# A Swin block on one core: the four turns of a round set behind each other, the other fillers placed singly

## The reference, cut to what matters

```python
shortcut = x
y = _ln(x, norm1_w, norm1_b)
y = jnp.roll(y, (-SS[0], -SS[1]), axis=(1, 2))
...
qkv = (win @ qkv_w.T).reshape(B * nW, N, 3, h, d).transpose(2, 0, 3, 1, 4)
q, k, v = (qkv[0], qkv[1], qkv[2])
attn = jnp.einsum('bhnd,bhmd->bhnm', q, k) * scale
...
attn = jax.nn.softmax(attn.reshape(B * nW, h, N, N), axis=-1)
out = jnp.einsum('bhnm,bhmd->bhnd', attn, v).transpose(0, 2, 1, 3).reshape(B * nW, N, C)
out = out @ proj_w.T + proj_b
...
x = shortcut + out
z = _ln(x, norm2_w, norm2_b)
z = jax.nn.gelu(z @ fc1_w.T + fc1_b, approximate=False) @ fc2_w.T + fc2_b
return x + z
```

## Time and profile before

| | |
|---|---|
| median of 3 runs | 2226.96 us (2225.48 to 2228.99) |
| the profiled execution | 2222.98 us |
| its span | 2221.2 us |
| granted TensorE clock over the span | 0.991 |
| busy share: TensorE, its weight loads, VectorE, ScalarE, GpSimd | 97%, 75%, 79%, 70%, 80% |

### The profile page before, as it was taken

The page is one execution under the profiler, slowest core; times in us unless marked ns, Lnnn a source line. Parts: engine busy times, 40 slices in busy tenths (PEclk is TensorE's granted clock), DMA queues, the critical chain, the costliest instruction groups (busy, mean ns, idle before and its releaser), DMA issues.

```text
span 2221.2 us, 147938 instructions
## 1 busy us (share of the span) xinstructions
PE 2147.9 (97%) x62756; PEld 1670.2 (75%) x62756; DVE 1748.1 (79%) x3231; ACT 1546.9 (70%) x2435; POOL 1770.5 (80%) x1687
## 2 busy tenths in 40 slices
PE   4999999999999999999999999999999999999997
PEld 3777777777777777777777777777777777777775
DVE  5778887887887888788788788878878887887874
ACT  3577777677677677767767767776776777677675
POOL 5788888888888888888888888888888888888874
PEclk7999999999999999999999999999999999999999
DMA  4232322222323332332333223222223323322321
GB/s 109 64 76 76 76 75 75 76 76 74 77 75 76 75 75 76 73 78 75 76 76 74 76 74 76 75 74 76 75 75 77 73 75 75 75 76 74 77 67 35
DMA packets 178587, 165.86 MB, mean 75 GB/s; under 512 B 21144, under 2 KB 152458, under 8 KB 178074
## 3 DMA queue, kind: packets, MB, share of 16 engines
q1 hardware_dynamic: 178074, 157.60, 28.1%
HBM read 28.99 MB, written 25.77 MB: 25 GB/s over the span
## 4 chain that ended last, share of the span: by engine, by line
PE 83%; ACT 9%; issue 4%; SPq 2%; DVE 1%; DMA 1%; ACTq 0%; POOL 0%; DVEq 0%; POOLq 0%
PE O L749 13%; PE ST L735 10%; PE M L757 9%; PE S L713 9%; PE ST L729 8%; PE M L842 8%; PE M L820 6%; PE M L789 5%; PE M L805 5%; PE M L775 5%; ACT L445 5%; ACT gl L445 4%; PE M L850 3%; PE S L717 1%; SPq L274 1%
## 5 line engine op out<-in xcount | busy, mean ns | idle before, releaser
L326 POOL TENSOR_TENSOR nmd<-diag,nm 121x392 f16<-121x392 f16 x1024 | 898.3, 886 | 320.5 <-DVE nm L582 310.4
L582 DVE TENSOR_REDUCE nm<-S 121x8 f16<-121x392 f32 x1024 | 576.2, 563 | 276.2 <-PE S L713 151.9
L426 ACT ACTIVATE pT<-ST 113x392 f32<-113x392 f32 x1024 | 506.4, 495 | 309.9 <-PE ST L735 305.2
L749 PEld LDWEIGHTS O<-vx,pT 113*49 113x49 f32 x16384 | 547.5, 126 | 43.2 <-issue 3.2
L749 PE MATMUL O<-vx,pT 113*49 113x18 f32 x16384 | 521.3, 196 | 0.9 <-DVE on L592 0.9
L713 PE MATMUL S<-kp,qp 128*49 128x49 f16 x16384 | 387.7, 186 | 16.1 <-DVE nm L582 8.1
L729 PE MATMUL ST<-qp,kp 128*49 128x49 f16 x16384 | 386.6, 185 | 4.1 <-ACT pT L426 2.1
L713 PEld LDWEIGHTS S<-kp,qp 128*49 128x49 f16 x16384 | 313.4, 104 | 86.6 <-issue 60.2
L735 PE MATMUL ST<-nmd,shiftw 121*49 121x392 f16 x2048 | 356.8, 345 | 0.1
L729 PEld LDWEIGHTS ST<-qp,kp 128*49 128x49 f16 x16384 | 323.9, 103 | 13.3 <-issue 2.7
L735 PEld LDWEIGHTS ST<-nmd,shiftw 121*49 121x49 f16 x2048 | 107.9, 102 | 264.9 <-POOL nmd L326 130.7
(11 more groups left out here) (88 smaller groups left out, 3307.0 us busy)
## 6 DMA issues: line engine op xcount, KB each, us to landing
qp<-hl SPq DMA_DIRECT2D x1024, 49.0 KB
kp<-hl SPq DMA_DIRECT2D x1024, 49.0 KB
xin<-in_x SPq DMA_DIRECT2D x256, 98.0 KB
out<-res SPq DMA_DIRECT2D x256, 98.0 KB
kp<-in_c_keys SPq DMA_DIRECT2D x4, 588.0 KB, 7.3
weights<-in_c_weights SPq DMA_DIRECT2D x1, 448.0 KB, 5.3
bias_t<-spread SPq DMA_DIRECT2D x2, 73.5 KB, 2.2
shiftw<-in_c_shift SPq DMA_DIRECT2D x1, 139.0 KB
```

Of the source, the lines that this page charges most:

```text
L326: nc.gpsimd.tensor_tensor(nmd[j % LAG][:], diag[:], nm[j % LAG][:].unsqueeze(2).broadcast_to([RM, 2 * 4, N]), ALU.mult).then_inc(s_nmd, 1)
L426: nc.scalar.activation(pT[j % LAG][:].rearrange("k w h q -> k (w h q)"), ST[0:R, j % 2, 0:HK], ACT.Exp).then_inc(s_e, 1)
L582: V.tensor_reduce(nm[j % LAG][:], S[0:RM, 0:HK].rearrange("q (h n) -> q h n", n=N), AX_X, ALU.max, negate=True).then_inc(s_nm, 1)
L749: mm = MM(O[W0 * w:W0 * w + N, (4 * p + hp) * VC:(4 * p + hp + 1) * VC], pT[j % LAG][:, w, hp, :], vx[r % RING][:, window + 2 * w, hp, :], ...
```

## The change

The same arithmetic is done with the same instructions; only places, banks of M and the waits that guard the banks differ.

- TensorE: project_out moves from unit 6 to unit 0 of the next round, project_qk from the middle of unit 0 to its end, fc2 from unit 4 to unit 2 of the next round. All four turns stand behind each other in unit 4, in the order z, y, back, o. fc1 moves from units 2 and 3 to units 6 and 7 of the round before, high half first. Units 3 and 5 have no filler.
- VectorE: add_attention, ln2_center, ln2_var, evac_zT, evac_yT, result, ln1_var and the ln1 steps get other units; ln1_sum(n) now stands in unit 1 ahead of low_parts(a).
- GpSimd: keep_residual moves from unit 0 to unit 6; ln2_rstd and ln2_rows to unit 1, behind ln1_rows; ln1_rstd ahead of shift_rows in unit 7.
- ScalarE: exp comes first in its unit; gelu goes from unit 2 to unit 6, evac_m from 5 to 3, the squares to unit 4.
- SP: store(g) stands behind spread_parts(a) instead of ahead of it.

The diff, cut to the moves and the waits; the pieces left out renumber banks of M in operands.

```diff
@@ -283,11 +283,11 @@
                     load_constants()
                     load_keys(0)
                     spread_bias()
-                if on_chip(g):
-                    store(g, m)
                 if on_chip(a):
                     spread_parts(a, m + 1, 0)
                     spread_parts(a, m + 1, 1)
+                if on_chip(g):
+                    store(g, m)
                 if isinstance(i, int) and i == -1:
                     load_keys(1)
 
...
             def body(i, m):
-                f, n, d = i + 2, i + 3, i - 2
+                f, n, e = i + 2, i + 3, i - 3
                 if isinstance(i, int) and i == 0:
                     blank_values(2)
                     blank_values(3)
                     pool.wait_ge(c_const_in, 48)
                 for k in range(U):
-                    if k == 0 and on_chip(i):
-                        keep_residual(i, m)
+                    if k == 7 and on_chip(n):
+                        ln1_rstd(n)
                     if on_chip(i):
                         shift_rows(i, k)
-                    if k == 1 and on_chip(f):
-                        ln1_rows(f)
-                    if k == 4 and on_chip(d):
-                        ln2_rstd(d)
-                        ln2_rows(d)
-                    if k == 7 and on_chip(n):
-                        ln1_rstd(n)
+                    if k == 1:
+                        if on_chip(f):
+                            ln1_rows(f)
+                        if on_chip(e):
+                            ln2_rstd(e)
+                            ln2_rows(e)
+                    if k == 6 and on_chip(i):
+                        keep_residual(i, m)
 
...
             def gelu(u, c):
-                act.wait_ge(s_f, 2 * u + 1 + c)
-                if c == 0 and later(u):
+                act.wait_ge(s_f, 2 * u + 2 - c)
+                if c == 1 and later(u):
...
                     if isinstance(i, int) and i == 0 and k in (5, 7):
                         place_bias(1, k // 7)
+                    u, j = at_unit(i, k, 2)
+                    if on_chip(u):
+                        exp(u, j)
                     if k == 0 and on_chip(a):
                         high_parts(a, m + 1)
                     if k == 1 and on_chip(a):
                         place_v(a, m + 1)
-                    u, j = at_unit(i, k, 2)
-                    if on_chip(u):
-                        exp(u, j)
-                    if k == 0 and on_chip(d):
-                        square2(d)
-                    if k == 2 and on_chip(e):
+                    if k == 3 and on_chip(g):
+                        evac_m(g)
+                    if k == 4:
+                        if on_chip(c):
+                            evac_oT(c)
+                        if on_chip(d):
+                            square2(d)
+                        if on_chip(n):
+                            square1(n)
+                    if k == 6 and on_chip(e):
+                        gelu(e, 1)
                         gelu(e, 0)
-                        gelu(e, 1)
-                    if k == 3 and on_chip(n):
-                        square1(n)
-                    if k == 4 and on_chip(c):
-                        evac_oT(c)
-                    if k == 5 and on_chip(e):
-                        evac_m(e)
...
-                    if k == 0:
+                    if k == 0 and on_chip(c):
+                        normalise(c, 0)
+                    if on_chip(i):
+                        neg_max(i, k)
+                    if k == 0 and on_chip(d):
+                        add_attention(d, m + 2)
+                    if k == 1:
                         if on_chip(d):
                             ln2_sum(d, m + 2)
+                        if on_chip(n):
+                            ln1_sum(n, m + 3)
+                        if on_chip(a):
+                            low_parts(a)
+                    if k == 2 and on_chip(n):
+                        ln1_center(n, m + 3)
+                    if k == 3 and on_chip(c):
+                        normalise(c, 1)
+                    if k == 4:
+                        if on_chip(d):
+                            ln2_center(d, m + 2)
                         if on_chip(e):
                             evac_zT(e)
-                        if on_chip(c):
-                            normalise(c, 0)
-                    if k == 4 and on_chip(c):
-                        normalise(c, 1)
-                    if on_chip(i):
-                        neg_max(i, k)
-                    if k == 0:
-                        if on_chip(g):
-                            result(g, m)
-                        if on_chip(d):
-                            ln2_center(d, m + 2)
-                    if k == 1:
-                        if on_chip(a):
-                            low_parts(a)
+                    if k == 5 and on_chip(g):
+                        result(g, m)
+                    if k == 6:
+                        if on_chip(f):
+                            evac_yT(f)
                         if on_chip(d):
                             ln2_var(d)
-                    if k == 2 and on_chip(n):
-                        ln1_sum(n, m + 3)
-                    if k == 3 and on_chip(n):
-                        ln1_center(n, m + 3)
-                    if k == 4 and on_chip(f):
-                        evac_yT(f)
-                    if k == 5 and on_chip(n):
+                    if k == 7 and on_chip(n):
                         ln1_var(n)
-                    if k == 6 and on_chip(c):
-                        add_attention(c, m + 3)
...
-            def turn_y(u, e):
+            def turn_y(u, a):
                 pe.wait_ge(s_y1, u + 1)
-                if on_chip(e):
-                    pe.wait_ge(s_g, 2 * e + 1)
+                if on_chip(a):
+                    pe.wait_ge(s_lo, a + 1)
+                turn_tokens(0, y1, s_yTp)
+
+            def project_qk(u, g):
+                pe.wait_ge(s_yT, u + 1)
+                if on_chip(g):
+                    pe.wait_ge(s_g, 2 * g + 2)
                 elif later(u):
                     pe.wait_ge(s_lo, u)
-                turn_tokens(1, y1, s_yTp)
-
-            def project_qk(u, d):
-                pe.wait_ge(s_yT, u + 1)
-                if on_chip(d):
-                    pe.wait_ge(s_att, d + 1)
                 for h in range(2):
                     rows = slice(C * h, C * h + C)
                     mm = MM(M[:, h, 0:HT], wqk[rows, :], yT[rows, :], start=True, stop=True)
                 mm.then_inc(s_qk, 1)
 
-            def room_for_v(u, e, g):
-                if on_chip(e):
-                    pe.wait_ge(s_zT, e + 1)
+            def room_for_v(u, d):
+                if on_chip(d):
+                    pe.wait_ge(s_att, d + 1)
                 elif later(u):
                     pe.wait_ge(s_vx, 2 * u)
-                if on_chip(g):
-                    pe.wait_ge(s_res, g + 1)
 
             def project_v(u):
                 for s in range(8):
                     for e in range(2):
-                        mm = MM(M[W0 * e:W0 * e + N, 2, C * s:C * s + C], yT[:, N * s:N * s + N], wv[:, e, :],
+                        mm = MM(M[W0 * e:W0 * e + N, 3, C * s:C * s + C], yT[:, N * s:N * s + N], wv[:, e, :],
                                 start=True, stop=True, tile_position=(0, W0 * e))
                 mm.then_inc(s_vp, 1)
 
...
-            def turn_o(u, e, a):
+            def turn_o(u, d, g):
                 pe.wait_ge(s_on, 2 * u + 2)
-                if not on_chip(e):
-                    pe.wait_ge(s_vx, 2 * a + 2)
-                turn_tokens(3, on, s_oTp)
-
-            def project_out(u, f):
+                if on_chip(g):
+                    pe.wait_ge(s_mT, g + 1)
+                elif on_chip(d):
+                    pe.wait_ge(s_oT, d + 1)
+                turn_tokens(2, on, s_oTp)
+
+            def project_out(u, i, g):
                 pe.wait_ge(s_oT, u + 1)
-                if on_chip(f):
-                    pe.wait_ge(s_yT, f + 1)
+                if on_chip(g):
+                    pe.wait_ge(s_g, 2 * g + 1)
+                elif on_chip(i):
+                    pe.wait_ge(s_vx, 2 * i + 2)
                 for q in range(4):
                     for w in range(2):
-                        mm = MM(M[W0 * w:W0 * w + N, 0, 2 * C * q:2 * C * q + 2 * C], oT[:, q, W0 * w:W0 * w + N], wproj,
+                        mm = MM(M[W0 * w:W0 * w + N, 3, 2 * C * q:2 * C * q + 2 * C], oT[:, q, W0 * w:W0 * w + N], wproj,
                                 start=True, stop=True, tile_position=(0, W0 * w))
                 mm.then_inc(s_pj, 1)
...
-            def turn_z(u, e, a):
+            def turn_z(u, a, d):
                 pe.wait_ge(s_z1, u + 1)
-                if on_chip(e):
-                    pe.wait_ge(s_mT, e + 1)
-                else:
+                if on_chip(a):
                     pe.wait_ge(s_vx, 2 * a + 2)
```

(84 more changed lines are left out.)

8 lines of the change are left out of this document (3 added, 5 removed).

## The result

| | before | after |
|---|---|---|
| median | 2226.36 us (4 runs) | 2356.89 us (4 runs, 2354.41 to 2360.32) |
| ratio to before | | 1.0596, 95% interval 1.0582 to 1.0611 |
| span of the profiled execution | 2221.2 us | 2355.6 us |
| mean granted TensorE clock | 0.991 | 0.971 |
| mean round, between low_parts and low_parts | 16.84 us | 17.89 us |

The forecast was slower, 2288 us, with 2230 to 2345 as its range. The sign and the mechanism were right. The forecast growth was 61 us and the measured one 130.5, so the size was a little under half of what came, and 2357 us lies above the range.

What follows compares the result with a forecast made beforehand. TensorE's work bounds the kernel before; after the change SP's ring does, at 1.07 + 11.04 + 0.5 + 1.64 + 2.35 + 0.59 = 17.19 us. Growth of 0.50 us in 122 rounds, 61 us, gives 2288 us, range 2230 to 2345.

Steps and rivals of the forecast that it cites:

- SP's ring: Low_parts, spread_parts, store, load, ln1_sum, back to low_parts: each waits for the one before, 17.19 us a round in the mean.
- the landing of the load: From the last issue of SP's load to its data: taken as 2.35 us, between 1.78 and 2.53.
- The round before: TensorE's round in the unchanged kernel, from one first half of fc1 to the next: 16.69 us.
- slow issues: SP's sixteen spread_parts issues: 10.47 us in a quick round, 10.9 to 12.9 in 44 of 105 rounds, mean 11.04.
- Rival 2: Ring and TensorE both meet near the old round, 16.65 to 16.75 us: 2222 to 2231 us; chance 0.06.
- The turns: Four transposing turns joined on TensorE save 0.27 us of entries and 0.2 us at their ends each round.
- TensorE's own round with its waits: TensorE's work of 15.9 us plus new waits of 0.2 and 0.3: 16.4 us, between 16.0 and 16.7.
- The wait of project_out for the gelu: On TensorE in unit 0, project_out waits about 0.3 us for the bank that the gelu frees.
- Rival 1: SP's ring does not bind and TensorE's 16.4 us round stands: 2190 us, or 2143 with waits hidden; chance 0.10.
- rival 3: TensorE's clock falls in its waits, 3.4 us each: 2398 us, or 2315 at most if one in four does; chance 0.13.
- Rival 4: The four joined turns, 2.0 us of only transposes, drop TensorE's clock by themselves every round: 2605 us; chance 0.02.
- Nothing at zero cost: Edits priced at nothing: new bank order, moved GpSimd and VectorE steps; thin cover only at ln2_rows ahead of turn_z, 0.1 to 0.9 us.

Runs made afterwards that it cites:

- e1: Changed kernel with one swap: low_parts ahead of ln1_sum again in VectorE's unit 1; 2198.41 us, 0.988 of the kernel before.
- e3: Changed kernel with only SP's order altered: the store of a round goes behind the next round's load; 2211.98 us, 0.994 of the kernel before.
- e6: Kernel of e1 with turn_o taken out of the chain of turns into unit 5, evac_oT with it; 2241.05 us, 1.009 of the kernel before.
- e5: Changed kernel with both e1's swap on VectorE and e3's order of SP; 2180.13 us, 0.981 of the kernel before.
- e4: Kernel before with two moves: SP's store behind spread_parts, ln1_sum in VectorE's unit 1 ahead of low_parts; 2379.76 us, ratio 1.071.

## Why the prediction was half right

**SP's ring closes and sets the round: right**, by the waits of ln1_sum, by e1 and by e3. The order of events is the one told, step for step: ln1_sum waits for its load, low_parts and the row maximum of unit 2 stand behind it, the scores of unit 3 wait.

**The size of the ring: 17.19 forecast, 17.93 measured.** The step that failed is the landing of the load. I put it at 2.35 us between ends of 1.78 and 2.53; it took 2.96 in the mean (2.93 where VectorE is seen to wait), and its upper end was too low. That is 0.61 of the 0.74 us. I had two rows for it: the end of the traffic, which is no landing, and one wait at the start of the kernel. Neither shows the spread. In steady state the quickest of 106 landings took 2.20 us and the slowest 4.44. By e3 the store in front makes an estimated 0.2 of it. In two rounds read in short stretches (the last section has the rows) the data come 0.6 and 0.5 us behind the end of the traffic, and the traffic ends 2.2 and 3.1 us behind the last issue, where the row that I used had 1.78: in them it is the traffic that takes longer. Why it does stays open. The other terms were close: 1.09 for 1.07, 10.97 for 11.04, 0.59 for 0.5 of steps, 1.73 for 1.64 of store and load, 0.60 for 0.59.

**The round before: 16.69 taken, 16.84 in the mean.** I read one quick round and set it against a mean of the ring with its slow issues in. The other way round from the landing, this made the forecast 0.15 us a round too high. And I had counted 122 rounds, where the mean growth holds for 127. Rival 2's upper end has an error of its own: by the same sum 16.75 us a round make 2234 us, not 2231. Together: 0.50 x 122 = 61 us forecast, 1.05 x 127 = 133 measured.

**The turns: right, and worth more.** I had 0.27 us for entries and 0.2 for the ends. The trace of e1 has 1.75 us for the four turns joined, against 3 x 0.54 + 0.62 + 3 x 0.09 = 2.51 before: 0.76 us saved. e6 prices one join at 0.23, 0.69 for three.

**TensorE's own round with its waits: 16.4 forecast.** e1, without the ring, has quick rounds of 16.2 (from 1001.24 to 1017.46 at the shift behind the turns) and a mean of 16.66; e5 has 16.48. Forecast and mean can't be set against each other for the reason told above, but the gains can: 16.69 - 16.4 = 0.29 us were forecast, and from before to e5 the mean fell by 16.84 - 16.48 = 0.36. The wait of project_out for the gelu is there: in e1 it follows scores_T after 0.52 us (1006.95, 1007.47) and not after the 0.30 of fc1. Rival 1, the same kernel if the ring did not bind, was put at 2190 us; e5, where it does not, has 2180.

**The clock: a small part.** The mean granted clock fell from 0.991 to 0.971, as rival 3 has it in its mild form. In the changed kernel it is below 1.00 in 23 of the 106 rounds, and 20 of these, at 0.82 to 0.91, are rounds in which ln1_sum does not wait for its load; in the kernel before no round of this stretch has such a fall. Two long waits of TensorE at unit 3:

```profile
372.20 0.40 PE L715 MATMUL S<-kp,qp 128*49 128x49 f16 x16 [1.91 <-DVE nm L584]
```

```profile
746.01 0.45 PE L715 MATMUL S<-kp,qp 128*49 128x49 f16 x16 [2.11 <-DVE nm L584]
```

Behind the first the clock stays at 1.00. Stretches behind the second, columns as in rows 8:

```profile
746.00:747.00 1.00, 0.99 (x36) 0.97 (x38) 0.88 (x2) 0.00 (x0) 0.88 (x1) 0.60 0.05 11
747.00:748.00 1.00, 1.00 (x30) 0.90 (x28) 0.27 (x2) 0.57 (x2) 0.93 (x2) 0.50 0.33 89
748.00:749.00 1.00, 1.00 (x33) 0.79 (x28) 0.96 (x3) 0.41 (x1) 0.16 (x1) 0.50 0.25 62
749.00:750.00 1.00, 1.00 (x8) 1.00 (x9) 0.90 (x3) 0.00 (x0) 0.66 (x1) 0.69 0.34 89
```

0.50 is 1.2 GHz instead of 2.4. This fall takes 0.40 + 0.50 + 0.50 + 0.31 = 1.7 us of TensorE's time, the price that rival 3 had for a round. The slack in the ring takes nearly all of it: in the 20 rounds ln1_sum starts 3.13 us behind the last issue, against 2.93 where it waits. As an estimate the falls cost 20 x 0.2 = 4 us in this stretch, and 19 at most, if all 20 loads had landed after the quickest 2.20.

Rival 4 is refuted: e1 and e5 have the same chain of turns at clocks of 0.989 and 0.993. The rule of the Trainium skill that a transpose does not count as activity (TensorE: Matmul & The Clock Gate, Part 4: PE-mode transpose) thus shows in no clock here, with 1.75 us of nothing but transposes in each round. These runs do not contradict it either, since the wait of 1.91 us above left the clock at 1.00 as well.

**Nothing at zero cost was missed on GpSimd.** z1 comes in time: in the round shown of the changed kernel turn_z follows scores_T after the usual 0.30 us (1018.07 - 1017.77).

## What to carry to other kernels

When steps are moved, follow each transfer from its issue to its first reader and on to what the next issue waits for; if the path comes back to where it began, add its terms up, since a step that is hidden in both places can close a ring that is not. Then count the waits that name it: neighbouring stretches of a trace always add up, ring or not. Here two neighbours in one queue of VectorE were worth 158 us. Price a landing from many waits in steady state or give it a wide end, and set means against means: a quick round compared with a mean of anything else is off by what the slow rounds cost. Test such a ring by taking one element out of it that touches no other engine, as the store in e3; moving a step on the busy engine, as in e4, changes two things at once.

## What the runs showed of the hardware

**Where traffic ends, a transfer has not landed.** Stretches of the changed kernel (columns as in rows 8) around a load whose last issue ended at 1010.71 and whose reader started at 1013.51:

```profile
1012.50:1012.75 0.25, 0.25 (x27) 0.25 (x24) 0.00 (x0) 0.25 (x1) 0.25 (x2) 1.00 0.41 156
1012.75:1013.00 0.25, 0.23 (x17) 0.13 (x10) 0.00 (x0) 0.25 (x2) 0.25 (x1) 1.00 0.12 41
1013.00:1013.25 0.25, 0.23 (x13) 0.23 (x14) 0.00 (x0) 0.25 (x1) 0.25 (x1) 1.00 0.02 8
```

The data stop at about 1012.9, 2.2 us behind the last issue, and VectorE, which waits for them, starts at 1013.51, 0.6 us later. In the next round the last issue ended at 1028.11 and the reader started at 1031.76:

```profile
1029.75:1030.00 0.25, 0.25 (x12) 0.24 (x10) 0.25 (x1) 0.00 (x0) 0.16 (x1) 1.00 0.27 74
1030.00:1030.25 0.25, 0.25 (x16) 0.22 (x10) 0.25 (x1) 0.00 (x0) 0.25 (x1) 1.00 0.05 8
1031.00:1031.25 0.25, 0.25 (x4) 0.09 (x2) 0.00 (x0) 0.25 (x1) 0.25 (x1) 1.00 0.05 16
1031.25:1031.50 0.25, 0.25 (x6) 0.06 (x4) 0.00 (x0) 0.23 (x2) 0.25 (x1) 1.00 0.00 0
```

Most of the data are there by 1030.0, a thin rest goes on to 1031.25, 3.1 us behind the last issue, and the reader starts 0.5 us behind that.

The Trainium skill (DMA: Bandwidth & Descriptors, Anatomy of one DMA) gives about 2.0 us of fixed cost and the bytes at 436 GB/s, for another issuing path; worked out from these, an estimate for a load of 98 KB is 2.2 us. That is the quickest landing seen here, not the mean of 2.96.

**VectorE and GpSimd: a step's time depends on what runs beside it.** The small scaling of ln2_var, 113 x 8 elements, took 0.54 us in the mean before and takes 0.93 after. Groups of VectorE before and after; the last line is the same operation for ln1 after:

```profile
L621 DVE TENSOR_SCALAR veps<-ss 113x8 f32<-113x8 f32 x128 | 68.9, 538 | 4.4
```

```profile
L623 DVE TENSOR_SCALAR veps<-ss 113x8 f32<-113x8 f32 x128 | 119.2, 931 | 4.4
L564 DVE TENSOR_SCALAR veps<-ss 113x8 f32<-113x8 f32 x128 | 22.0, 172 | 4.4
```

In order of time, GpSimd's keep_residual and this step in the changed kernel:

```profile
1005.51 1.27 POOL L346 TENSOR_TENSOR xres<-xin,projb 113x512 f32<-113x512 f32 x1
...
1005.86 0.96 DVE L623 TENSOR_SCALAR veps<-ss 113x8 f32<-113x8 f32 x1
```

It ends at 1006.82, just behind GpSimd's 1006.78. The same operation for ln1, which stands beside no GpSimd step (1025.68, GpSimd's next begins at 1025.93), takes 0.17. GpSimd's times move too: keep_residual took 1.60 us in its old place and takes 1.27 now. The Trainium skill (SBUF — State Buffer, Who interferes with whom) says that the two share a pair of ports which one instruction holds to its end, and that it takes a VectorE step of certain modes, or one with two inputs in SBUF, to want it; the rows of ln2_var agree, though no run here was made to test it. None of these steps is a term of the ring. Still, what stands beside what on these two engines is a term of its own when steps are dealt anew: I had given moved steps the durations of their old places.
